# Self attention of a decoder layer: the scale of the probabilities on VectorE instead of GpSimd

## What is computed

```python
q = apply_rope((x @ wq).reshape(b, s, H, HD), cos, sin)      # H=16, HD=128, s=512
k = apply_rope((x @ wk).reshape(b, s, KV, HD), cos, sin)     # KV=4, each for 4 heads
scores = jnp.einsum('bqhd,bkhd->bhqk', q, k) / np.sqrt(HD)
scores = jnp.where(causal[None, None], scores, jnp.finfo(scores.dtype).min)
probs = jax.nn.softmax(scores, axis=-1)
out = jnp.einsum('bhqk,bkhd->bqhd', probs, v).reshape(b, s, H * HD) @ wo
```

## Time and profile before

| | us |
|---|---|
| three executions | 1495.98, 1500.64, 1494.89 (median 1495.98) |
| the profiled execution | 1488.05 |
| its span | 1485.9 |
| self attention's steps in that span | about 738 to 1052 |

### The profile page before, as it was taken

One profiled execution on the slowest core, in us unless ns is written; L12 is line 12 of the kernel. 1 busy time (PEld: TensorE's weight loads), 2 busy tenths in 40 slices (PEclk: granted clock), 3 DMA queues, 4 the chain that ended last, 5 costly groups with the idle time before them and its releaser, 6 DMA issues. The chain is left out here.

```text
span 1485.9 us, 25011 instructions
## 1 busy us (share of the span) xinstructions
PE 1370.9 (92%) x8027; PEld 726.2 (49%) x8027; DVE 1026.3 (69%) x1918; ACT 812.9 (55%) x1437; POOL 370.2 (25%) x586
## 2 busy tenths in 40 slices
PE   7988999999999999996779999998769999999996
PEld 4444444444444444433345555554345665555663
DVE  5847777777777777787478887887567455555565
ACT  5546666666666666675166665657434434444432
POOL 5402020202020202023365654643143000000042
PEclk9999999999999999997789999999879999999998
DMA  8227777676767676883653535355747566646571
GB/s 249 51 65 127 149 114 148 113 149 113 148 113 148 113 148 113 161 155 86 220 108 62 136 66 135 58 104 101 178 163 231 174 210 229 204 148 199 177 193 58
DMA packets 455085, 208.74 MB, mean 140 GB/s; under 512 B 403232, under 2 KB 417568, under 8 KB 455008
## 3 DMA queue, kind: packets, MB, share of 16 engines
q1 hardware_dynamic: 451872, 199.43, 56.5%
q0 software_dynamic: 2560, 8.39, 1.8%
q10 hardware_dynamic: 576, 0.00, 0.0%
HBM read 88.23 MB, written 17.83 MB: 71 GB/s over the span
## 5 line engine op out<-in xcount | busy, mean ns | idle before, releaser
L1440 DVE SCALAR_TENSOR_TENSOR X<-xa_SC,xa_rs,X 128x1024 f16<-128x1024 f32 x128 | 164.3, 1283 | 98.7 <-issue 98.0
L1264 ACT ACTIVATE X<-xa_SC,xa_rs 128x1024 f16<-128x1024 f32 x128 | 147.1, 1149 | 110.6 <-POOL xa_rs L1001 110.6
L1139 PE MATMUL xa_psS<-xa_KT,xa_QT 128*128 128x512 f16 x768 | 186.4, 379 | 6.3 <-DVE xa_mn L1472 4.9
L1151 PE MATMUL xa_psO<-wide,xa_V 128*128 128x512 f16 x768 | 173.8, 383 | 7.1 <-DMA wide<-X 7.1
L1001 POOL TENSOR_SCALAR xa_rs<-xa_rc,flag 128x1 f32<-128x1 f32 x128 | 34.2, 267 | 517.3 <-DVE xa_rc L1433 517.3
L1472 DVE CUSTOM_DVE_ANT_0 xa_SC<-xa_psS,maskb 128x1024 f32<-128x1024 f32 x128 | 154.9, 1210 | 4.6 <-PE xa_psS L1139 2.4
L1286 ACT ACTIVATE xa_SC<-xa_SC,xa_mn 128x1024 f32<-128x1024 f32 x128 | 145.4, 1136 | 13.4 <-DVE xa_mn L1472 13.3
L1876 PE MATMUL rmoe_psG<-rmoe_XGT,W 128*128 128x352 f16 x768 | 125.8, 314 | 5.6 <-DVE causal L1996 3.6
L1891 PE MATMUL rmoe_psY<-W,rmoe_HT 128*128 128x512 f16 (+1 forms) x576 | 125.9, 379 | 0.3 <-DVE rmoe_HT L2001 0.3
L1876 PE MATMUL rmoe_psU<-rmoe_XGT,W 128*128 128x352 f16 x768 | 125.9, 314 | 0.0
L1151 PEld LDWEIGHTS xa_psO<-wide,xa_V 128*128 128x128 f16 x768 | 74.6, 99 | 102.7 <-issue 17.7
(11 more groups left out here) (258 smaller groups left out, 2292.1 us busy)
## 6 DMA issues: line engine op xcount, KB each, us to landing
first<-in_L_ffn_w_dram SPq DMA_DIRECT2D x14, 2048.0 KB, 11.9
W2raw<-in_L_ffn_w_dram SPq DMA_DIRECT2D x8, 2048.0 KB, 8.9
expert_rows_dram<-zeros SPq DMA_DIRECT2D x11, 512.0 KB, 8.9
xa_WPraw<-in_L_xattn_Wq_dram SPq DMA_DIRECT2D x8, 512.0 KB, 4.8
xa_WOraw<-in_L_xattn_Wo_dram SPq DMA_DIRECT2D x8, 512.0 KB, 4.6
first<-in_L_ffn_wq_dram SPq DMA_DIRECT2D x4, 1024.0 KB, 7.4
first<-in_L_ffn_wo_dram SPq DMA_DIRECT2D x4, 1024.0 KB, 5.5
first<-in_L_ffn_w_dram SPq DMA_DIRECT2D x8, 512.0 KB, 5.5
```

The source lines that it names most:

```text
L1139: last = nc.tensor.matmul(psS[j % NSC][:, c:c + cw], QT[b][:, hq, g, t * P:(t + 1) * P], KT[b][:, hk, c:c + cw], start=(q == 0), stop=(q = ...
L1151: last = nc.tensor.matmul(psO[:, c:], V[b][:, hv, blk, :], PT[g % NPT][:, blk, hp, c:], start=(blk + q == 0), stop=(blk == NBLK - 1 and q ...
L1264: nc.scalar.activation(PN[j % NPN][:, 0:w // P, 0, :], by_block(SC[j % NSC], w), ACT.Identity, scale=rs[:, j % 4:j % 4 + 1]).then_inc(norm ...
L1440: nc.vector.scalar_tensor_tensor(out=PN[j % NPN][:, 0:w // P, 1, :], in0=by_block(SC[j % NSC], w), scalar=rs[:, j % 4:j % 4 + 1], in1=PN[j ...
```

## The change

In self attention POOL no longer computes the scale. DVE does it, directly behind the reciprocal, with a wait for the reciprocal between them. In cross attention POOL keeps its scale.

```diff
@@ POOL, half() @@
-                    pool.wait_ge(recip_done, n + 1)
-                    wait_from(pool, split_done, n - 3)
-                    stand_apart(pool, pool_passed)
-                    unit = PSCALE if flag is None else flag[:, b:b + 1]
-                    nc.gpsimd.tensor_scalar(rs[:, j % 4:j % 4 + 1], rc[:, j % 4:j % 4 + 1], unit, 1.0, ALU.mult,
-                                            ALU.mult).then_inc(scale_done, 1)
+                    if not causal:
+                        pool.wait_ge(recip_done, n + 1)
+                        wait_from(pool, split_done, n - 3)
+                        stand_apart(pool, pool_passed)
+                        nc.gpsimd.tensor_scalar(rs[:, j % 4:j % 4 + 1], rc[:, j % 4:j % 4 + 1], flag[:, b:b + 1], 1.0,
+                                                ALU.mult, ALU.mult).then_inc(scale_done, 1)
@@ DVE @@
+            def scale(n, j):
+
+                dve.wait_ge(recip_done, n + 1)
+                wait_from(dve, split_done, n - 3)
+                stand_apart(dve, dve_passed)
+                nc.vector.tensor_scalar(rs[:, j % 4:j % 4 + 1], rc[:, j % 4:j % 4 + 1], PSCALE, None,
+                                        ALU.mult).then_inc(scale_done, 1)
@@ DVE, half() @@
                     if causal and m < NS and (m >= 0 or not first):
                         reciprocal(n - SUM_LAG, m)
+                        scale(n - SUM_LAG, m)
```

## The result

| | before | changed |
|---|---|---|
| executions, median (lowest to highest), us | 1500.65 (1494.89 to 1501.99), 6 | 1529.22 (1525.86 to 1534.35), 6 |
| the profiled execution and its span, us | 1488.05, 1485.9 | 1527.61, 1526.0 |

The ratio is 1.0197, with a 95% interval from 1.0176 to 1.0218. The change costs 2%, some 29 us. It was forecast at 0.3%.

What follows compares the result with a forecast made beforehand. PE was taken to bound the kernel, with DVE setting its waits at wo(0). 3.6 + 4.2 - 3.0 - 0.5 = +4.3 us on the median 1495.98 gave 1500.3 us (+0.3%), range 1489 to 1512.

Steps and rivals of the forecast that it cites:

- What bounds the kernel: Whole kernel: PE bounds it; DVE's five steps from step 2's mask set PE's wait at wo(0), six times.
- Part 1: DVE, self attention: the scale behind the reciprocal adds 0.20 us a step; +3.6 us, bounds 0 and 6.0.
- The gap: Step 5, DVE: 0.52 us idle ahead of the low half of 512, absorbing 0.4 of 1.0 us a half.
- Part 2: DVE beside POOL, ahead of wo(0): the scale is held by POOL's instructions, 0.7 us a half; +4.2 us.
- if the scales all last 0.15 us: Sign in the new profile: scales never lasting 0.3 to 1.2 us would show the +4.2 us of holding wrong.
- the low half is held rarely now: Argument against the slower rival: DVE's low half has a mean of only 611 ns.
- Part 3: Odd halves: POOL without 128 scales runs ahead, DVE's wait for rope_low goes; -3.0 us, bounds 0 and 5.7.
- Part 4: First and last half: earlier weight piece, chain without POOL; -0.5 us, bounds -3 and +2.
- POOL's freedom costs more: Self attention, DVE: scale and low half held one after the other, DVE full; +14 us, 1510; chance 0.34.
- waits at `psS`: Sign for the slower rival: PE waiting at psS for the mask, as its four score tiles no longer cover DVE.

Runs made afterwards that it cites:

- POOL paced: The changed kernel, with POOL again waiting for each step's reciprocal and scaling a constant into a tile that nothing uses; 1.0158 of the kernel before.
- untied: The kernel before, POOL's scale kept, plus a 128 x 1 DVE instruction behind each self attention reciprocal that waits for nothing and writes a spare tile; 1.0042.
- tied: The kernel before, POOL's scale kept, plus a second scale on DVE with the changed kernel's waits and semaphore, into a tile that nothing uses; 1.0218.
- the run with one wait less: The changed kernel, its DVE scale waiting for the reciprocal alone, without the second wait and the semaphore step; 1.0122 of the kernel before.

## Why the prediction was wrong, step by step

- **What bounds the kernel.** Right. DVE's stream between step 2's mask and wo(0) sets the end, six times, and 25.6 of the 27.4 us lie at these six places. The claim of where to look held; the sizes did not. That five steps lie ahead of each wo(0) is right for halves 2, 3 and 5, but in half 4 it is seven.
- **Part 1, the scale's place on DVE** (+3.6 us, upper end 6.0). The failed step is the 0.20 us a step. It measured 0.44. The 0.20 came from a chain in the router with one wait between small instructions; the scale has two waits and a semaphore step, which the diff shows, and the low half behind it has its own. Once the engine stands at an unmet wait, everything behind it is exposed: 0.19 us from reciprocal to scale with one wait, 0.34 with the other wait and the step; 0.17 from scale to low half, 0.26 with one wait more. The gap absorbed a little more than the 0.4 that I gave it (4 x 0.44 - 0.18 = 1.6 remain of 2.2). At 1.6 us a half the part would be +9.5 us; with half 4's two further steps, a longer wait in half 6 and 2.1 us in half 1 it is up to 11.9, the six waits of the changed kernel with POOL paced. Here I cited the Trainium skill (VectorE: DVE Perf Modes, "The DRAIN you can't avoid"), by which a semaphore between two VectorE instructions costs nothing extra; the page has measured it on a row of tensor copies. The runs disagree for a 128 x 1 instruction: untied 1.0042, tied 1.0218.
- **Part 2, what the scale meets on POOL** (+4.2 us). Wrong in its mechanism, and near in its size by luck. The scale is never held: of the 128 none took over 0.16 us, although 49 started in the middle of a long POOL instruction. By my own test ("if the scales all last 0.15 us") this part was wrong. But POOL's freedom did cost, through the low halves: 0.75 us in half 2, where I had said 0.7. Over the six waits parts 2 and 3 together make +2.8 us, where I had +1.2, and with the slower products behind the waits 0.4 of a hundredth over the whole, some 6 us. My reading of the earlier trace rows, that a held low half runs after POOL has ended, was a little off as well: it ended 0.14 us behind POOL, not 0.33. My reason against it, that "the low half is held rarely now", described the kernel before, in which POOL's scale kept it so. The Trainium skill (SBUF — State Buffer, "Who interferes with whom") has that an instruction with at most one SBUF input stays clear of GpSimd outside the two-port modes, and that one with two such inputs contends with a GpSimd instruction that reads SBUF. This trace agrees with the second (low half 1.04 for 0.60), and the scale's 0.15 to 0.16 us agree with the first; in which mode the scale ran, no run shows.
- **Part 3, POOL relieved** (-3.0 us). The relief came as foretold, and was more than eaten up. DVE's 2.1 us of waits for `rope_low` are at 0.0, but the waits at wo(0) of odd halves went from 1.89 to 3.83 us instead of shrinking: in half 3 the chain took 1.6 and the longer low halves 1.2, against the 1.05 that the wait gave.
- **Part 4, the edges** (-0.5). Over self attention what is left beside the six wo(0) is 27.4 - 25.6 = +1.8 us. PE's 2.1 us wait for a weight piece did go, while a wait for transposes in the last half grew from 4.38 to 5.91.
- **What had no part at all:** PE's clock, 11 of the 29 us, and with part 1 the step that failed. I priced a microsecond of PE's wait as a microsecond. In the kernel before the waits of up to 1.89 us at wo(0) were all followed by products of 2.76 us, but one row of that trace shows the price: behind a wait of 2.08 us in half 0 the twelve products of line 1083 take 4.45 us. I had used that wait in part 4 and not read the duration beside it.

```profile
772.38 4.45 PE L1083 MATMUL sa_psJ<-XT,first 128*128 128x512 f16 x12 [2.08 <-POOL first L975]
```

- **The rivals.** "POOL's freedom costs more" had the right side and a part of the mechanism, at 1510 of the old median, +14 us; its sign for deciding it, waits at `psS`, isn't what happened (PE's waits at `psS` for the mask are 3.3 us over all of self attention). The range reached to 1512; on the same footing the time was 1496 x 1.0197 = 1525. Nothing in it had room for the clock.

With the sizes measured the 27.4 us of self attention are: the chain up to 11.9, where I had 3.6; POOL's freedom 2.8, longer low halves less its relief, where I had 1.2; slower products 11.0, where I had nothing; the rest 1.8. The first two are told apart by the run with POOL paced, in which two low halves are still held, for 0.7 and 0.3 us, and the last is a remainder.

## What to carry to other kernels

Before an instruction is tied to the one just ahead of it on the same engine, count every wait and semaphore step behind it until the next long instruction: here the small instruction with its waits and steps added 0.44 us a step, where 0.20 was priced. Behind a low half the same second wait and step cost about half as much (0.33 us in half 2 instead of 0.65), and the stand-still at the reciprocal was gone. An engine that is relieved starts its long instructions at other moments, and what it then overlaps can cost more than the relief gives; a small wait that looks useless may be the brake that keeps two engines apart. And a wait of PE is priced with the products behind it, by a row of the trace that shows them.

## What the runs showed of the hardware

- PE's clock did not follow the length of the wait alone. With the untied instruction two waits of the same length, in halves 3 and 5, ended differently:

```profile
880.05 4.45 PE L1108 MATMUL sa_psJ<-sa_WO,sa_OT 128*128 128x512 f16 x12 [2.09 <-DVE sa_OT L1492]
...
966.76 2.76 PE L1108 MATMUL sa_psJ<-sa_WO,sa_OT 128*128 128x512 f16 x12 [2.09 <-DVE sa_OT L1492]
```

  A wait of 2.88 us was followed by 2.76 us of products, in the run with one wait less, and one of 2.60 by 4.38. All six waits of the changed kernel, 3.24 us and more, were followed by the lower clock.
- A low half held by a POOL instruction that was under way ended 0.14 us behind it at a width of 128, 0.28 at 256, 0.41 at 384 and 0.55 at 512, give or take 0.03 us, in every profile of this case. Alone it takes 0.33, 0.47, 0.60 and 0.75 us. So all but its first 0.19 to 0.20 us came behind POOL's end, whenever it had started.
- A small instruction on DVE hides its duration but not its dependence: 0.13 us long, it moved what followed by 0.05 us untied and by 0.28 to 0.53 us tied.
- A DVE instruction of one element per partition with one tensor input and a constant was not slowed by POOL once in 128, 49 of which started inside a long POOL instruction; one with two tensors in SBUF beside the same POOL instructions was.
